# Up-weight casts cut by block, a one-block first load, and a reordered first tile

## The reference

```python
def _qlinear(x, q, scale, A, Bm):
    w = (q.astype(jnp.float32) - Q_ZERO) * (scale * Q_STEP)[:, None]
    y = jnp.einsum('bsh,oh->bso', x, w)
    return y + LR_SCALE * (x @ A @ Bm)
g = _qlinear(x, gate_q, gate_scale, gate_A, gate_B)
u = _qlinear(x, up_q, up_scale, up_A, up_B)
h = jax.nn.silu(g) * u
return _qlinear(h, down_q, down_scale, down_A, down_B)
...
x = x + 0.5 * _L0_ffn_ref(_layernorm(x), ...)
x = x + _L0_attn_ref(_layernorm(x), ...)      # y = irfft(rfft(u) * rfft(K)) + D * u
x = x + 0.5 * _L0_ffn_ref(_layernorm(x), ...)
```

## Time and profile before

| | |
|---|---|
| median of 3 runs | 561.35 us (561.17 to 561.72) |
| profiled execution, its own time | 561.36 us |
| span in its trace (first to last instruction) | 559.5 us |
| TensorE busy | 551.3 us, 99% of the span |
| VectorE, ScalarE, GpSimd busy | 75%, 56%, 47% |
| time that TensorE waits for another engine, whole span | 4.2 us, all of it before 45.3 us |

### The profile page before, as it was taken

One profiled execution on the slowest core, in us unless ns is written; L12 is line 12 of the kernel. 1 busy time (PEld: TensorE's weight loads), 2 busy tenths in 40 slices (PEclk: granted clock), 3 DMA queues, 4 the chain that ended last, 5 costly groups with the idle time before them and its releaser, 6 DMA issues.

```text
span 559.5 us, 12687 instructions
## 1 busy us (share of the span) xinstructions
PE 551.3 (99%) x4814; PEld 449.3 (80%) x4814; DVE 419.1 (75%) x807; ACT 312.9 (56%) x773; POOL 262.4 (47%) x295
## 2 busy tenths in 40 slices
PE   7999999999999999999999999999999999999997
PEld 7644678897788877888778887788877888788975
DVE  6789988986898857988579885798755987545544
ACT  5677525863278732787327872278722775256621
POOL 4379623873347730477304773047730486015510
PEclk9999999999999999999999999999999999999999
DMA  8996531008050390003800038000482004440002
GB/s 266 336 294 209 84 64 25 2 1 133 19 22 1 65 154 11 2 2 68 150 11 1 2 67 151 11 2 1 54 164 84 3 2 62 86 156 2 2 0 77
DMA packets 91434, 39.79 MB, mean 71 GB/s; under 512 B 79756, under 2 KB 85517, under 8 KB 91373
## 3 DMA queue, kind: packets, MB, share of 16 engines
q1 hardware_dynamic: 90397, 38.64, 31.8%
q10 hardware_dynamic: 976, 0.34, 0.3%
HBM read 15.64 MB, written 4.19 MB: 35 GB/s over the span
## 4 chain that ended last, share of the span: by engine, by line
PE 94%; DVE 3%; ACT 1%; DMA 1%; issue 1%; DVEq 0%; SPq 0%; ACTq 0%
PE banks L1627 42%; PE banks L1546 29%; PE banks L1589 6%; PE banks L1603 5%; PE banks L1771 5%; PE banks L1498 2%; PE banks L1566 2%; DMA X<-in_x 1%; PE banks L1583 1%; PE banks L1791 1%; PE banks L1557 0%; ACT work L766 0%; PE banks L1481 0%; DVE ring L1115 0%; DVE z L978 0%
## 5 line engine op out<-in xcount | busy, mean ns | idle before, releaser
L1627 PE MATMUL banks<-xT,w 128*128 128x256 f16 (+1 forms) x2156 | 259.6, 273 | 0.2
L1627 PEld LDWEIGHTS banks<-xT,w 128*128 128x128 f16 (+1 forms) x2156 | 212.7, 100 | 24.0 <-issue 0.7
L1546 PE MATMUL banks<-dw,hT 128*128 128x256 f16 (+3 forms) x1408 | 183.9, 286 | 0.0
L1546 PEld LDWEIGHTS banks<-dw,hT 128*128 128x128 f16 (+1 forms) x1408 | 135.4, 98 | 33.6 <-DVE work L1103 0.3
L1074 DVE SCALAR_TENSOR_TENSOR work<-banks,work 128x512 f32<-128x512 f32 (+1 forms) x88 | 60.6, 689 | 49.7 <-PE banks L1589 33.3
L615 POOL TENSOR_SCALAR hT<-work 128x512 f16<-128x512 f32 x70 | 43.5, 621 | 99.4 <-DVE work L1074 98.4
L618 POOL TENSOR_TENSOR hT<-work,hT 128x512 f16<-128x512 f32 x70 | 81.6, 1166 | 5.8
L1088 DVE SCALAR_TENSOR_TENSOR banks<-banks,scales,work 128x512 f32<-128x512 f32 (+1 forms) x77 | 57.7, 750 | 1.0 <-PE banks L1627 0.7
L1095 DVE SCALAR_TENSOR_TENSOR banks<-banks,scales,work 128x512 f32<-128x512 f32 (+1 forms) x77 | 57.7, 750 | 0.2 <-ACT work L857 0.2
L857 ACT ACTIVATE work<-banks,scales 128x256 f32<-128x256 f32 (+1 forms) x77 | 36.5, 473 | 36.4 <-PE banks L1627 36.3
L625 POOL TENSOR_TENSOR z<-zs,z 128x1024 f16<-128x1024 f32 (+1 forms) x28 | 53.8, 1926 | 3.8 <-ACT z L790 3.7
(11 more groups left out here) (196 smaller groups left out, 675.5 us busy)
## 6 DMA issues: line engine op xcount, KB each, us to landing
out_x<-X SPq DMA_DIRECT2D x15, 256.0 KB, 2.8
X<-in_x SPq DMA_DIRECT2D x1, 2048.0 KB, 10.2
ring<-in_gate_q_t SPq DMA_DIRECT2D x2, 768.0 KB, 9.1
hT<-in_up_q_t SPq DMA_DIRECT2D x2, 768.0 KB, 10.6
X<-in_b SPq DMA_DIRECT2D x2, 560.0 KB, 10.8
X<-in_x SPq DMA_DIRECT2D x1, 1024.0 KB, 14.0
ring<-in_down_q_t SPq DMA_DIRECT2D x1, 1024.0 KB, 13.5
X<-in_x SPq DMA_DIRECT2D x3, 256.0 KB, 5.1
```

Of the source, the lines that this page charges most:

```text
L1546: last = mm(acc(j)[:, 1 - c, 0:width], hT[0:rows[m], m, a, j * P:(j + 1) * P], dw[0:rows[m], m, src], start=(m == 0 and a == 0), stop=(m = ...
L1627: last = mm(dst[0:r, 0:HH], w[:, blocks + k, cols], xT[:, a, 2 * op + k, :], start=(first and k == 0 and a == 0), stop=(k == 1 and a == 1) ...
```

## The change

The first chunk of blocks (0, 1) is split into two chunks of one block. `cast_up` now casts one block at a time, eleven in all; `cast_up(0)` and `cast_up(1)` stay in the start, and after block `m` of tile 0, `m` from 0 to 4, come blocks 2; 3; 4 and 5; 6 and 7; 8, 9 and 10. The semaphore `s_ucast` counts blocks. The scaling of group 3 of tile 0 moves from VectorE to GpSimd, between the last root and the second gate cast. GpSimd subtracts the low-rank A parts after two roots, not after three. ScalarE copies group 0's transposes out before it makes group 1's high part, and `cast_up(0)` stands after `p_high(0, 0)`. TensorE has 92 warm products, not 124, and runs `p_product(0, 0)` and later `first_products(0)` earlier in its list.

```diff
-CHUNKS = [(0, 2), (2, 5), (5, 8), (8, 11)]
+CHUNKS = [(0, 1), (1, 2), (2, 5), (5, 8), (8, 11)]
...
             for c in range(2):
-                chunk(c)
+                chunk(0 if c == 0 else 2)
+                if c == 0:
+                    chunk(1)
...
-            ln_rstd(0, 0, 1, 2)
+            ln_rstd(0, 0, 1)
             pool.wait_ge(s_ahi, 2)
             pool.tensor_tensor(a_w[:, :, 2 * R:4 * R], a_raw, a_w[:, :, 0:2 * R], ALU.subtract).then_inc(s_aw, 1)
+            ln_rstd(0, 2)
+            cast_gate(0)
             ln_rstd(0, 3)
-            cast_gate(0)
+
+            pool.wait_ge(f.zs, 3)
+            pool.wait_ge(f.z16, 2)
+            pool.wait_ge(f.rstd, 4)
+            pool.tensor_scalar(zs_plain[:, 1, :], X[:, 3, :], meanvar[:, 3, 0:1], rstd[:, 3, :],
+                               ALU.subtract, ALU.mult).then_inc(f.zs, 1)
             cast_gate(1)
+            cast_gate(2)
...
-                    if n == 0 and m in (2, 4):
-                        cast_up(1 + m // 2)
+                    if n == 0 and m < 5:
+
+                        for ahead in ((2,), (3,), (4, 5), (6, 7), (8, 9, 10))[m]:
+                            cast_up(ahead)
...
-            def cast_up(c):
+            def cast_up(m):
+
+                c = sum(m >= m1 for _, m1 in CHUNKS)
+                at, r = (m - CHUNKS[c][0]) * P, rows[m]
                 act.wait_ge(s_q[c], 32)
-                cols = slice(CHUNKS[c][0] * P, min(CHUNKS[c][1] * P, I))
-                nc.scalar.activation(uw[:, :, cols], up_raw[c], ACT.Copy, bias=-Q_ZERO)\
+                nc.scalar.activation(uw[:, :, m * P:m * P + r], up_raw[c][:, :, at:at + r], ACT.Copy, bias=-Q_ZERO)\
                     .then_inc(s_ucast, 1)
...
             z_first_high(0)
             low_rank_a_high()
+            x_out(0, 0, 2)
             z_first_high(1)
-            x_out(0, 0, 2)
+            p_high(0, 0)
             cast_up(0)
             z_first_high(2)
-            p_high(0, 0)
             z_first_high(3)
             p_high(0, 1)
+            x_out(2, 2, 2)
             low_rank_b_high(0)
             low_rank_b_high(1)
-            x_out(2, 2, 2)
...
             ln_scale(0, 2)
+            p_split(0, 0)
             x_out(1, 1, 3)
-            ln_scale(0, 3)
             ln_low(0, 2)
             ln_low(0, 3)
-            p_split(0, 0)
+            p_split(0, 1)
             x_out(3, 3, 3)
-            p_split(0, 1)
```

More of the change, by code:

```diff
@@ L378, in _ @@
                 sp.dma_start(vct[:, :, at], state_d[:, 9:].rearrange("n (c m) -> n c m", c=2)).then_inc(s_kin, 16)
-            chunk(2)
+            chunk(3)
             sp.dma_start(X[:, TS:2 * TS, :], x_v[:, TS:2 * TS, :]).then_inc(s_xrest[0], 16)
@@ L387, in _ @@
                 sp.dma_start(part, at).then_inc(s_lrd, 16)
-            chunk(3)
+            chunk(4)
             for part, (m0, m1) in zip(dq_early, ((0, 4), (4, DQ))):
@@ L637, in _ @@
                     .then_inc(s_bhi[g], 1)
-            cast_gate(2)
+            cast_gate(3)
             s4_real_parts()
             ln_rstd(1, 0, 1)
-            cast_gate(3)
+            cast_gate(4)
             ln_rstd(1, 2, 3)
@@ L1345, in weight_sum @@
                     if i < 2 and k == 0:
-                        dve.wait_ge((s_gcast, s_ucast)[i], len(CHUNKS))
+                        dve.wait_ge((s_gcast, s_ucast)[i], (len(CHUNKS), M)[i])
                     after(dve, s_wsum, (0, 0, 2, 6)[i])
@@ L1599, in product @@
                 if n == 0:
-                    pe.wait_ge((s_gcast, s_ucast)[g], 1 + sum(m >= m1 for _, m1 in CHUNKS))
+                    pe.wait_ge((s_gcast, s_ucast)[g], (1 + sum(m >= m1 for _, m1 in CHUNKS), m + 1)[g])
                 for c in range(KH):
@@ L1795, in first_products @@
                         last.then_inc((f.g_mm, f.u_mm)[g], 1)
-            warm(96)
+            warm(72)
             x_transpose(0, 0, 2)
-            warm(28)
-            x_transpose(1, 1, 3)
+            warm(12)
             pe.wait_ge(s_aw, 1)
             p_product(0, 0)
+            warm(8)
+            x_transpose(1, 1, 3)
+            first_products(0)
             p_product(0, 1)
-            first_products(0)
             x_transpose(2, 2, 2)
```

## The result

The changed kernel takes 562.02 us (median of 20 runs, 561.32 to 562.97), the kernel before 561.32 us beside it (20 runs, 560.49 to 562.09). The ratio is 1.0015, 95% interval 1.0008 to 1.0021: 0.70 us more, 0.45 to 1.18 by the interval. The forecast was 561.9 after 561.36. The profiled execution took 562.08 us with a span of 560.3; before, 561.36 and 559.5.

The account below looks back on a forecast made before the run. Omega's landing, through GpSimd, VectorE and ScalarE, was taken to set TensorE's block 7 gate product at 45.25 us. Loads +0.5, casts and warm products 0, the start's 0.6 gain not arriving: 561.36 + 0.5 = 561.9 us, 8-in-10 range 560.8 to 562.9.

Parts of the forecast that it names:

- the chain: Omega's landing, GpSimd, VectorE, ScalarE, then TensorE's gate product of block 7 at 45.25 us, forecast to move to 45.75.
- the start: TensorE's first full-width products in tile 0: forecast at 19.2 us instead of 19.81, 0.6 us earlier, not reaching 45.25.
- The price of one instant: The whole change is worth exactly what it moves the start of block 7's gate product, at 45.25 us.
- The threshold for the start, 20.8: With the chain at 45.75 us, TensorE's full-width products can start as late as 20.8 us without mattering.
- the term: Loads of the first chunk: 2048 pieces of 512 bytes for 1024 of 1024 make omega 0.5 us later.
- the price line: DMA cost per piece, 46.8 ns at 1024 bytes and 66.2 at 1536, giving 27.4 ns at 512 bytes.
- the 0.4 us that I allowed: On the way the chain can lose or win about 0.4 us where VectorE's and GpSimd's operations meet differently.
- the two engines get in each other's way: VectorE and GpSimd share a port pair, so `ln_low(0, 2)` waits for GpSimd's scaling and starts at 13.55 us.
- The pair of durations: The same VectorE scaling of 512 numbers took 0.546 us once, 1.699 beside GpSimd's 1.37 us cast.
- The casts and the warm products: ScalarE's seven extra up-cast operations, 1.1 us more but hidden, and TensorE's 32 fewer warm products: each summed to 0.
- Rival C: TensorE's clock falls to 1.2 GHz in the start, full-width products begin at 22.7: 563.8 us; chance 0.08.
- Rival D: First-chunk loads: 512-byte pieces cost as much as 1024-byte ones, omega 3.0 us later: 564.4 us; chance 0.05.

Follow-up runs that it names:

- the roots first: Kernel before with GpSimd's roots of the next tile ahead of the last two additions of s4_real_parts: 561.47 against 561.11 us, ratio 1.0003.
- the fill: Changed kernel with one tiny unread memset (0.06 us) added at the start of VectorE's list: 561.69 against 561.11 us, ratio 1.0009.

## Why the prediction was right, and where not

**What bounds the kernel: right.** In the changed kernel block 7's gate product moved with every link of the chain, and the start did not matter: 0.2 us won there, 0.39 lost at 45 us. The price of one instant was right too for a loss. It was wrong as a general sentence. "The whole change is worth exactly what it moves one instant" holds only for moving it later; moved 0.27 us earlier, with the roots first, the next bound stood at 59 us, within half a microsecond, and I had read no row behind 45.3 us because TensorE doesn't wait there. The threshold for the start, 20.8, was too simple as well. It takes TensorE's way from the start to block 7 as fixed. With the smaller pieces alone that way had a new wait of 0.40 us at block 4, so a start of 20.32 made TensorE free at 45.67, not at 45.30; it held in the kernel with the old chunks (46.26 for 46.29).

**The loads: right in kind, short in size.** 0.5 us was the term. `omega`'s first use moved 0.63. Over all traces in which its place in the queue is unchanged, it was at 30.21 to 31.14 in the seven with the old first chunk, and at 31.46 to 32.11 in the six with the 512-byte pieces. The medians, 31.0 and 31.7, are 0.7 us apart, where the price line from 1024 and 1536 bytes said 0.5. What the chain did with it on the way was within the 0.4 us that I allowed: 0.63 at `omega` became 0.39 at the roots, since GpSimd took 6.30 us from the one to the other where it had taken 6.54 before.

The Trainium skill (DMA: Bandwidth & Descriptors, Specifications) puts 512 bytes at line rate. No trace here agrees: 294 and 342 GB/s in 6 to 10 us, against 350 and 360.

**The start: right side, wrong step.** 19.60, not 19.2. Two errors met. GpSimd's scaling took 2.09 us, not 1.64, and began at 12.28, not 11.9, because the last root stood in front of it. And it did not hold up `ln_low(0, 2)`:

```profile
12.89 0.69 DVE L992 TENSOR_TENSOR z<-zs,z 128x512 f16<-128x512 f32 x1
15.06 0.69 DVE L992 TENSOR_TENSOR z<-zs,z 128x512 f16<-128x512 f32 x1 [1.48 <-ACT z L913]
```

The first row is `ln_low(0, 2)`, at its usual 0.69 us in the middle of the scaling (12.28 to 14.37); the second is `ln_low(0, 3)`, which waits for the scaling's result by way of ScalarE. So group 2's transposes came at 13.63, before my 14.25, and group 3's at 15.81 behind 0.66 us of idle. The step that failed is the one from "the two engines get in each other's way" to "therefore this operation waits". The Trainium skill (SBUF — State Buffer, on the port pair) has an operation of VectorE with two SBUF inputs block against one of GpSimd that reads SBUF. This pair did not; the times of the weight sums beside `z_low` fit it. The pair of durations that I had read as agreeing with it fits less well than I wrote: the scaling of 1.699 us began at 38.76, 0.05 us ahead of the cast and not behind it.

**The casts and the warm products: right.** The casts alone gave a ratio of 0.9998, and the granted clock stayed at 1.00 through holes that left 1.29 us of work in 2. Rival C had 0.08 and never began. Rival D, 3.0 us at `omega`, is excluded by 0.63.

**The waits: fewer than forecast at block 7, and one behind that I had not.** I had written that TensorE would wait 1 to 2 us around blocks 6 and 7. It waits 0.52 us there where it waited 0.30; the rest of the 1.2 us lies at 24.87 (0.47) and 33.05 (0.23). "A new wait of TensorE behind 46 us, which I have no case for" is what came, 0.27 us at 152.3. In the trace my own mechanism gives 0.39 us at block 7 and 0.36 at the end (the lateness of the kernel with VectorE's scaling), and what I had not seen gives the other 0.43 of 0.79. So the agreement of 562.02 with 561.9 is in part luck. Three kernels without the second step (the pieces alone, 1.0007; the changed kernel with VectorE's scaling and that with the fill, 1.0009 each) show what the forecast was about: 0.5 to 0.6 us, with intervals that begin at no change.

## What to carry to other kernels

When a load is cut into smaller pieces so that its first part is used sooner, follow everything behind it in the same queue to the instant that sets the end, and price the smaller pieces by two sizes that the trace already shows. A wait removed on the critical path is worth only the distance to the next one, which the bounding engine's waits don't show: look one or two stages on for an operation whose margin is smaller than the gain, above all where VectorE and GpSimd share the work. A new operation ahead of a result that another engine waits for must not stand behind a load: with the unsplit chunk the same order cost 1.5 us in the start.

## What the runs showed of the hardware that I had not expected

- Two VectorE sums or differences of 1376 numbers, 0.86 us each alone, took 3.2 to 3.9 us beside one GpSimd subtraction of 1024 numbers (2.45 to 2.63 us), and 2.23 when it came after them.
- GpSimd's scaling of 128x512 by two per-partition values takes 2.09 us, the same with VectorE idle and with VectorE at work: 3.6 ns a number above the 0.24 us of its smallest operation, where one such value cost 2.73 and constants 0.79.
- A VectorE subtraction with both inputs in SBUF ran in its usual 0.69 us beside that scaling.
- VectorE can stand idle for 0.28 to 0.47 us with nothing to wait for that the profile shows, at a few places in a list of some 800 operations. The places differ between nearly equal kernels, and in one trace an empty operation 142 us earlier removed the one that cost time.
- The first use of `omega`, which waits for its load, differs by up to 0.9 us between kernels whose loads are identical (30.21 to 31.14; six of the seven lie within 0.25).
